# Attention with two PSUM banks for scores and three for maxima, and the fills of maxima spread over the positions of a pair

## The reference

```python
x = x + attn_a(layernorm(x))   # 32 query heads of 16, 8 key/value heads, rotary embedding, causal softmax
x = x + ffn(layernorm(x))      # 4-bit weights as codes, rank-32 corrections, silu(g) * u
x = x + attn_b(layernorm(x))   # 32 heads of 16, biases, causal softmax
x = x + ffn(layernorm(x))      # the same weights as the first ffn
# inside both attentions:
scores = jnp.einsum('bhqd,bhkd->bhqk', q, k) / math.sqrt(hd)
scores = jnp.where(causal, scores, -inf)
ctx = jnp.einsum('bhqk,bhkd->bhqd', softmax(scores), v)
```

## Time and profile before

| | before |
|---|---|
| median of 3 runs | 2312.54 us (2306.46 to 2316.6) |
| profiled execution | 2314.97 us |
| its span, first to last instruction | 2313.2 us |
| PE busy | 1910.5 us, 83% of the span |
| DVE busy | 1205.1 us, 52% |
| ACT busy | 933.7 us, 40% |
| POOL busy | 474.0 us, 20% |
| mean granted clock of PE | 0.929 of full speed |

### The profile page before, as it was taken

The page is one execution under the profiler, slowest core; times in us unless marked ns, Lnnn a source line. Parts: engine busy times, 40 slices in busy tenths (PEclk is TensorE's granted clock), DMA queues, the critical chain, the costliest instruction groups (busy, mean ns, idle before and its releaser), DMA issues. The chain is left out here.

```text
span 2313.2 us, 38681 instructions
## 1 busy us (share of the span) xinstructions
PE 1910.5 (83%) x13648; PEld 1359.7 (59%) x13648; DVE 1205.1 (52%) x2472; ACT 933.7 (40%) x1674; POOL 474.0 (20%) x1256
## 2 busy tenths in 40 slices
PE   3887988978985899996488888788888886799998
PEld 3554655645643677774356655555665654577775
DVE  4665565665553755542444644554464453655543
ACT  3344444444432544541344443443444342445432
POOL 3212221221200211212122211221232120212211
PEclk9899999999988899998689899999999998799999
DMA  2000010010003520111100100000000101530110
GB/s 92 1 1 2 24 34 1 24 34 1 26 12 96 155 73 14 41 37 63 61 1 1 29 1 29 10 19 29 1 19 1 37 1 55 163 107 1 54 37 19
DMA packets 45986, 81.48 MB, mean 35 GB/s; under 512 B 6634, under 2 KB 17514, under 8 KB 45300
## 3 DMA queue, kind: packets, MB, share of 16 engines
q1 hardware_dynamic: 45812, 79.13, 10.9%
HBM read 62.34 MB, written 16.78 MB: 34 GB/s over the span
## 5 line engine op out<-in xcount | busy, mean ns | idle before, releaser
L252 PE MATMUL f_ring<-f_xt,f_codes 128*128 128x512 f32 (+1 forms) x1408 | 360.8, 399 | 23.8 <-DVEq L1314 22.0
L252 PEld LDWEIGHTS f_ring<-f_xt,f_codes 128*128 128x128 f32 (+1 forms) x1408 | 262.9, 188 | 95.8 <-DVEq L1314 23.4
L718 ACT ACTIVATE ab_region<-ab_scores 128x512 f32<-128x512 f32 x320 | 190.2, 600 | 141.6 <-PE ab_scores L898 140.6
L718 ACT ACTIVATE aa_region<-aa_scores 128x512 f32<-128x512 f32 x320 | 185.0, 598 | 128.7 <-PE aa_scores L898 124.7
L803 DVE TENSOR_REDUCE ab_nmax<-ab_maxima 128x1 f32<-128x384 f32 (+1 forms) x256 | 149.1, 620 | 143.6 <-PE ab_maxima L898 141.2
L1180 POOL TENSOR_TENSOR f_ht<-f_work,f_ht 128x512 fp32r<-128x512 f32 (+1 forms) x88 | 114.5, 1305 | 485.9 <-ACT f_ht L1239 485.9
L1325 DVE TENSOR_TENSOR f_work<-f_ring,f_work 128x512 f32<-128x512 f32 (+1 forms) x176 | 120.6, 690 | 154.8 <-ACT f_work L1228 126.0
L1228 ACT ACTIVATE f_work<-f_ring,f_scales 128x512 f32<-128x512 f32 (+1 forms) x176 | 120.8, 686 | 181.5 <-PE f_ring L252 181.1
L252 PE MATMUL f_ring<-f_dcodes,f_ht 128*128 128x512 f32 (+1 forms) x704 | 176.3, 405 | 10.2 <-DVE f_down_x L1303 9.3
L897 PE MATMUL aa_maxima<-aa_stacks 96*128 96x128 bf16 (+3 forms) x512 | 145.1, 329 | 41.9 <-DVE aa_nmax L803 28.3
L252 PEld LDWEIGHTS f_ring<-f_dcodes,f_ht 128*128 128x128 f32 (+1 forms) x704 | 133.0, 192 | 48.4 <-DVE f_down_x L1303 12.8
(11 more groups left out here) (185 smaller groups left out, 3652.9 us busy)
## 6 DMA issues: line engine op xcount, KB each, us to landing
f_x<-mid SPq DMA_DIRECT2D x32, 256.0 KB, 4.2
f_raw<-mid SPq DMA_DIRECT2D x32, 256.0 KB, 4.4
f_raw<-in_gate_q SPq DMA_DIRECT2D x10, 512.0 KB, 5.7
f_raw<-in_up_q SPq DMA_DIRECT2D x10, 512.0 KB, 5.0
f_raw<-in_down_q SPq DMA_DIRECT2D x10, 512.0 KB, 3.8
aa_x<-in_x SPq DMA_DIRECT2D x16, 256.0 KB, 3.1
aa_res<-in_x SPq DMA_DIRECT2D x16, 256.0 KB, 2.9
mid<-aa_res SPq DMA_DIRECT2D x16, 256.0 KB, 2.1
```

The lines of the kernel that those rows point to most:

```text
L252: mm = pe.matmul(out, w, x, start=start and i == 0, stop=stop and i == len(pairs) - 1)
L718: act.activation(probs[:, s // 2 % 2, SUB * (s % 2) + i, :], scores[:, sbk, :], ACT.Exp, scale=0.25).then_inc(scores_freed[sbk].sem, 1)
```

## The change

PSUM is divided anew: two banks for scores (three before) and three for maxima (two before). The bank of a chunk of scores is now its running number modulo two, the bank of a fill k modulo three. In the first attention the fills m0 to m3 move to positions 0 to 3, one in each (before, the six stood in positions 2, 3 and 4, two in each); the positions of the transposes and of the copy stay. In the second attention m4 and m5 of the pair that comes next stand in positions 0 and 1 (before, both in 0); m0 to m3 stay in positions 3 and 4; the transposes move from position 2 to 3 and the copy from 3 to 4. No instruction of computation is added or removed.

```diff
-        scores = ctx.enter_context(nc.psum_tensor(f"{name}_scores", [P, 3, EW], F32))
-        maxima = ctx.enter_context(nc.psum_tensor(f"{name}_maxima", [P, 2, EW], F32))
+        scores = ctx.enter_context(nc.psum_tensor(f"{name}_scores", [P, 2, EW], F32))
+        maxima = ctx.enter_context(nc.psum_tensor(f"{name}_maxima", [P, 3, EW], F32))
...
         if rope:
-            MAXIMA_AT = ((1, ()), (1, ()), (2, (0, 1)), (2, (2, 3)), (2, (4, 5)))
+            MAXIMA_AT = ((2, (0,)), (2, (1,)), (2, (2,)), (2, (3,)), (2, (4, 5)))
         else:
-            MAXIMA_AT = ((1, (4, 5)), (1, ()), (2, ()), (2, (0, 1)), (2, (2, 3)))
+            MAXIMA_AT = ((1, (4,)), (1, (5,)), (2, ()), (2, (0, 1)), (2, (2, 3)))
         FIRST = sum(len(ks) for ahead, ks in MAXIMA_AT if ahead == 2)
-        TRANSPOSE_AT, ROWS_AT, VALUES_AT = 2, 3, 4
+        TRANSPOSE_AT, ROWS_AT, VALUES_AT = 2 if rope else 3, 3 if rope else 4, 4
...
-                        sbk, nth = i % 3, SB[i % 3] * s + i // 3
+                        sbk, nth = (SUB * s + i) % 2, (SUB * s + i) // 2
...
-                mb, nth = k % 2, MB[k % 2] * s + k // 2
+                mb, nth = k % 3, MB * s + k // 3
...
-                pe.wait_ge(scores_freed[1].sem, scores_freed[1].at(b, SB[1] * (2 * n + 2)))
+                pe.wait_ge(scores_freed[1].sem, scores_freed[1].at(b, SUB * (n + 1)))
```

More of the change, by code:

```diff
@@ L457, in attention @@
         nmax_split = Signal(sem("nmax_split"), PAIRS, 1)
[L459 to L464, removed]
+        CHUNKS = SUB * PAIRS // 2
+        scores_filled = [Signal(sem(f"scores{i}_filled"), CHUNKS) for i in range(2)]
+        scores_freed = [Signal(sem(f"scores{i}_freed"), CHUNKS, 1) for i in range(2)]
+        MB = 2
+        maxima_filled = [Signal(sem(f"maxima{i}_filled"), MB * PAIRS) for i in range(3)]
+        maxima_freed = [Signal(sem(f"maxima{i}_freed"), MB * PAIRS, 1) for i in range(3)]
         av_made = Signal(sem("av_made"), QUADS, 4)
@@ L587, in split_max @@
                 nm, nr, np_ = nmax[:, s % 2], nrest[:, s % 2], nparts[:, s % 2]
-                pool.wait_ge(maxima_freed[1].sem, maxima_freed[1].at(b, MB[1] * (s + 1)))
+                pool.wait_ge(maxima_freed[2].sem, maxima_freed[2].at(b, MB * (s + 1)))
                 pool.wait_ge(rows_filled.sem, rows_filled.at(b, s - 1))
```

## The result

The changed kernel takes 2321.47 us (median of 13 runs, 2315.28 to 2325.52), the one before 2312.89 us in the same comparison (13 runs). The ratio is 1.0036, with a 95% interval from 1.0025 to 1.0048: slower by 0.36%, inside the 0.5% that was taken as "no change". The profiled execution has a span of 2316.0 us against 2313.2.

The account below looks back on a forecast made before the run. PE was taken as the fullest engine in both attentions, with only its waits able to move. From 2315 us: 40 less in the first, 39 more in the second, 2 for the clock, giving 2316 us; range 2276 to 2350.

Parts of the forecast that it names:

- hand-worked light pairs: First attention, pairs with few tasks: even ones 1.4 us shorter, odd ones 1.3; some 33 pairs, 45 us.
- Rival (d): First attention: two score banks hold PE behind ACT, so it gains 18 instead of 40 us; 2338 us, chance 0.13.
- (1): Second attention, first T hand-over: later m0 and the copy delay copying out; 1.1 us later, after 0.3 less for m5.
- (4): Second attention, values behind the T tasks: they wait 0.3 us more for the copy.
- the light pairs' 0.3: Second attention, a unit's two pairs without tasks: the moved copy makes them 0.3 us longer together.
- (2): Second attention, second T hand-over: only r4 stands in front of copying out; 0.6 us a unit back.
- (3): Second attention, third T hand-over: m5 and r5 now come ahead of copying out; 1.3 us a unit later.
- The clock, +2 forecast: Second attention, behind the T tasks: longer PE waits could lower its clock and add 2 us.
- Rival (a): Second attention hides the moved copy, losing only 5 to 10 us; 2280 us, chance 0.27.
- (b): Both attentions: a bank is what is missing, so fill waits end and moved transposes cost nothing; 2243 us, chance 0.05.
- (c): Second attention: T tasks lose more, 4.5 us a unit, 68 us in all; 2343 us, chance 0.20.
- (e): Whole kernel: the change does nothing and waits in both attentions keep their sums; 2315 us, chance 0.35 shared with the forecast.

Follow-up runs that it names:

- banks_only: Kernel before the change, with two score and three maxima banks in both attentions and all old positions kept: 2301.81 us, ratio 0.9955.
- first_and_banks: Changed kernel with every fill, transpose and copy of the second attention back in its old position, new banks kept in both: 2250.24 us, ratio 0.9729.
- m5_only: Changed kernel with the second attention's transposes and copy in their old positions, so only m5 is moved there: 2266.03 us, ratio 0.9807.
- t_filler: Changed kernel plus 20 unused matmuls ahead of the T task in positions 0 and 1 of each second-attention unit's third pair: 2287.68 us, ratio 0.9892.
- before_fillers: Kernel before the change plus unused matmuls in the second attention: 14 ahead of some transposes, 20 ahead of some T tasks: 2298.82 us, ratio 0.9948.

## Why the prediction was right or wrong

2316 us was forecast and 2321 measured; the sign of both large terms and their near-cancelling were right, and both were too small. That the total came so close is in part luck: the first attention was 13 us off, the second (with the 2 for the clock) 23 us the other way, and 8 us went outside the two windows (897 to 889), mostly in the unchanged ffn layers.

**First attention, 40 us less forecast, 53 measured.** The hand-worked light pairs came out as drawn: 7.1 and 6.2 us forecast, 7.06 and 6.11 measured. The 40 us is what the order and the banks gave without the clock (41 with the price of 0.26, 32 to 44 with those read in this attention). By parts it is less exact: the 32 light pairs that lie between two chunks e0 lost 47.5 us, with 43 us less half-clock time in them (some 36 without it, where 45 was said), and the other 31 pairs lost 5.9 where nothing, or a cost of 4, was said. What was left out is that the old order's waits held the clock down, which gave 12 us more by that price. The fills' wait fell below a third as said; that of the transposes to 14.0, not under 10.

**Rival (d) had a wrong mark.** "Chunks of scores waiting for ACT's L718 for over 15 us in all" came true (15.2 us, and 20.2 for the weight loads), and the attention was still shorter than forecast. So most of the wait may stand where PE had waited for something else before, which no run shows by itself; banks_only, with 18.6 us of it, suggests that in the old order it costs more. The length of the attention was the test, not the wait.

**Second attention, 39 us more forecast, 64 measured.** The mechanism was right: L1022's wait of 68.3 us (60 or more said), the new waits for L812. Without the clock it is 46. Steps (1), (4) and the light pairs' 0.3 stand for the transposes and the copy: with the 0.3 for m5 put back they make 2.0 us a unit, 30 us for 15 units, and 31 to 33 were measured. The step that was mis-sized is m5, (2) and (3): 0.3 + 0.6 gained and 1.3 lost, 0.4 us a unit or 6 us, where the runs show 20 to 22. Two things in it. DVE's second copying out did come 0.6 us sooner behind e0 (1.96 to 1.36 us), but PE's wait fell only from 1.70 to 1.47, as PE's own m5 had left that position too; and the third hand-over cost 1.47 us of waiting where 1.3 was said. That makes 1.47 - 0.3 - 0.23, about 0.9 us a unit or 14 us; read directly, from first_and_banks to m5_only, the pairs 6 without half clock grow by 0.7 us (12.3 to 13.0), or 10 us in all. The other 6 to 10 us lie at least partly in units whose later positions hold X and O, where I had seen no cost: in m5_only the pair 12 of a batch element grew from 11.1 to 12.9 us. The banks gave back 7 us (751 to 744) that I had not counted.

**The clock, +2 forecast, -12 and +18 by the price of 0.26.** This is the term that was furthest off. I had seen the half clock behind the T tasks and booked it as an afterthought, and only for the second attention. It went with the waits in both (83 to 36 us and 89 to 157 us at half clock), and it made up 18 of the 64 us in the second, which t_filler and before_fillers bear out, and between 9 and 21 of the 53 in the first, where it was not tested. That the two shares partly cancel is luck of the sum, not of the reasoning.

**Two slips in the working.** The fills' wait in the second attention was given as 31.7 us, which is the part for r0 and r1; with 8.3 us for L803 it is 40, so that the stall in the first was 2.3 times as large and not three times. Rival (a)'s sum takes off 43 us for the first attention where the forecast has 40. Neither changes the forecast.

**Rivals (a), (b), (c), (e).** (a) is out: the second attention is 64 us longer. (b) is out too: with the banks alone the whole kernel gains 0.45%, not the 3% of 2243 us; what the Trainium skill says of repeated gaps (Perfetto Trace Analysis, Optimization Strategy), that they can mean too few buffers, is borne out here only with the order that lets the third bank be used (17 us against 3). (c) came out for the second attention. Its mark of over 845 us was set from the 784 us of the earlier trace rows, which begins 9.6 us ahead of the first chunk of scores; cut like that, 838.3 is 848. The 64 us are 4.3 us a unit, past the 3.5 from which (c) was to decide, and nearer to its 4.5 than to my 2.4. Without the clock they are 3.1 a unit, so it takes the half clock, which (c) named, to get there. Its total of 2343 us missed because the first attention gained more than 40. (e) is out, since both attentions changed, though its total, 2315 us, fits as well as mine.

## What to carry to other kernels

Split a change by stage before judging it: this one was a gain of 2.2% and a loss of 2.9% in one edit, and the banks with the old order in the second attention give 2250 us (ratio 0.9729). Add to every wait you expect on PE, or expect to remove, what the clock does behind it: in the T tasks here a quarter of a microsecond for each microsecond at half clock (0.19 to 0.46 at other places), and it followed on three waits of about 1.5 us in 13 of 15 units. Price a half-clock stretch from two windows with the same work before you use it elsewhere. When moves seem not to add, take the clock out of the lengths first; what is left added within 2 us here.

## What was unexpected in the hardware

Useless matmuls inside PE's waits made the kernel faster: 600 of 128x128, 1.28 us for 20, took 112 us of half-clock time and 30.5 us off the second attention. The same kind of matmul where PE was not idle cost 0.8 us for each 14.

The half clock in the two attentions came in stretches of 3.4, 6.8 or 10.2 us, and the same pair of different units, with the same instructions, had 10.24 us of it or none. One unit's time therefore says little about the next. The sum over an attention was steadier: 89 and 93 us for the second attention of before, 157 and 160 for the changed one, each in two kernels; in the changed first attention it ran from 28 to 43.
